# A transformer block in float32: second token shift summed from ScalarE's outputs, unpadded LoRA row tiles, new instruction orders

## The reference, cut to what matters

```
xn  = ln(x);  sx = prev token of xn - xn
xxx = tanh((xn + sx*maa_x) @ maa_w1)            # 5 groups of 32
x5  = xn + sx*(maa_stack + xxx @ maa_w2)        # 5 mixtures: k, w, v, r, g
w   = exp(-exp(time_decay + tanh(x5[1] @ decay_w1) @ decay_w2))
r, k, v = x5[3] @ Wr.T, x5[0] @ Wk.T, x5[2] @ Wv.T;  g = silu(x5[4] @ Wg.T)
att = scan over time of s = k v + w s, read with r and u
x   = x + (groupnorm(att) * g) @ Wo.T
xn2 = ln(x);  sx2 = prev token of xn2 - xn2     # first token of a sequence: a row of the state
xk  = xn2 + sx2*ffn_maa_k;  xr = xn2 + sx2*ffn_maa_r
x   = x + sigmoid(xr @ ffn_Wr.T) * (relu(xk @ ffn_Wk.T)^2 @ ffn_Wv.T)
```

## Time and profile before

| | |
|---|---|
| time of three runs | 520.23, 521.76, 522.25 us; median 521.76 |
| span of the profiled execution | 520.3 us, first to last instruction |
| median less span | 1.46 us, what lies around the span and the spread of the runs |
| PE / DVE / ACT / POOL busy | 479.2 / 474.4 / 281.7 / 101.6 us |
| mean granted TensorE clock | 0.987 of full speed |

### The profile page before, as it was taken

One profiled execution on the slowest core, in us unless ns is written; L12 is line 12 of the kernel. 1 busy time (PEld: TensorE's weight loads), 2 busy tenths in 40 slices (PEclk: granted clock), 3 DMA queues, 4 the chain that ended last, 5 costly groups with the idle time before them and its releaser, 6 DMA issues. The chain is left out here.

```text
span 520.3 us, 6254 instructions
## 1 busy us (share of the span) xinstructions
PE 479.2 (92%) x2200; PEld 284.2 (55%) x2200; DVE 474.4 (91%) x528; ACT 281.7 (54%) x612; POOL 101.6 (20%) x93
## 2 busy tenths in 40 slices
...
DMA packets 26999, 69.49 MB, mean 134 GB/s; under 512 B 1624, under 2 KB 19928, under 8 KB 24536
## 3 DMA queue, kind: packets, MB, share of 16 engines
...
## 5 line engine op out<-in xcount | busy, mean ns | idle before, releaser
L630 DVE TENSOR_TENSOR_SCAN kv<-w_sb,kv 128x512 f32<-128x512 f32 (+2 forms) x144 | 146.6, 1084 | 0.1
L958 PE MATMUL pa<-x,large_sb 128*128 128x512 f32 (+2 forms) x272 | 115.2, 567 | 5.0 <-DVE x L545 2.9
L451 POOL COPY kv<-s_sb 128x32 f32<-128x32 f32 (+2 forms) x36 | 54.6, 1518 | 145.6 <-PE patt L1130 141.4
L958 PEld LDWEIGHTS pa<-x,large_sb 128*128 128x128 f32 x272 | 51.2, 194 | 57.5 <-issue 44.3
L620 DVE TENSOR_TENSOR kv<-vrep,k_sb 128x2016 f32<-128x2016 f32 (+2 forms) x34 | 70.1, 2064 | 3.3 <-issue 3.3
L638 DVE TENSOR_TENSOR kv<-kv,r_sb 128x2048 f32<-128x2048 f32 (+2 forms) x36 | 72.9, 2043 | 0.2
L536 DVE SCALAR_TENSOR_TENSOR x<-pb,vec_sb,sx 128x512 f32<-128x512 f32 (+1 forms) x64 | 42.7, 708 | 6.0 <-PE pb L1002 5.9
L420 POOL DMA_DIRECT2D x<-xn x21 | 20.0, 951 | 111.5 <-DVE x L536 111.5
L1130 PE MATMUL patt<-kv,const_sb 128*32 128x512 f32 (+2 forms) x288 | 34.7, 557 | 0.5 <-DVE kv L638 0.4
L1002 PE MATMUL pb<-th,w_sb 32*128 32x512 f32 (+2 forms) x100 | 33.3, 596 | 1.5 <-DVE x L536 1.5
L1156 PE MATMUL pc<-large_sb,att 128*128 128x256 f32 x120 | 32.0, 390 | 0.0
...
## 6 DMA issues: line engine op xcount, KB each, us to landing
...
x<-xn POOLq DMA_DIRECT2D x18, 512.0 KB, 8.3
...
x_tok<-in_x SPq DMA_DIRECT2D x6, 512.0 KB, 10.2
...
xres<-in_x SPq DMA_DIRECT2D x6, 512.0 KB, 10.7
out<-xres SPq DMA_DIRECT2D x6, 512.0 KB, 5.0
out<-trr POOLq DMA_DIRECT2D x6, 512.0 KB, 8.1
```

Of the source, the lines that this page charges most:

```text
L451: pool.tensor_copy(kv[:, q % 2, :, 0:nb, 0], s0_sb[:, half, G4 * j:G4 * (j + 1), FIRST[c]:FIRST[c] + nb]).then_inc(s0_put, 1)
L630: ins = dve.tensor_tensor_scan(flat, w_sb[:, p, q % HF, 0:nb].rearrange("p b t -> p (b t)"), flat, 0.0, ALU.mult, ALU.add)
L958: ins = pe.matmul(dst[:, m, 0:n], w(a)[:, m * P:(m + 1) * P], src[:, a, :], start=(a == 0), stop=(a == HF - 1))
```

## The change

`c_xn` now makes four tiles from the transposed norm in PSUM: for `xr` and for `xk` a part of the token itself (scale `ln2_w*(1 - m)`) and a part of the token before it (scale `ln2_w*m`, written one column later). That is eight ACTIVATEs in place of two and two small copies for the first tokens of the sequences. `c_shift` on DVE is one TENSOR_TENSOR that adds the two tiles of `xr`; for `xk` a DMA from POOL's queue adds them in SBUF (`add_shifted`, step ax), and KK waits for it; in the last three parts DVE adds `xk` too. The scale and bias vectors are made once on POOL (`make_vecs`, step mv, ten small instructions).

The fold of the fifth mixture goes from four quarters to two halves (`FOLD = 2`); the weights are no longer padded with zeros. X4 is four matmuls of 32 rows (`LORA`) and 256 columns, D2 four of 64 rows (`DECAY`) and 256 columns, and the two halves of the tokens go to different PSUM banks. All five order lists are replaced by lists that are written out in full. Because `k_shifted` lies where `xn2` lay and `r_shifted` lies in `sq`, xn2 now waits for Y2 of the chunk before. `load_v` waits for the stored v in both halves, since vl1 may now come first.

```diff
-FOLD, DFOLD = P // LORA, P // DECAY
+FOLD, DFOLD = 2, P // DECAY
...
-PE_ORDER = [("BO", 2), ("X2", 1), ("P0", 1), ("X3", 1), ("S0", 2), ("T2", 3), ("X4", 1), ("P1", 1), ("S1", 2),
-            ("RR", 3), ("D1", 1), ("KK", 3), ("D2", 1), ("P3", 1), ("Y2", 3), ("S2", 2), ("T1", 0), ("S3", 2),
-            ("CB", 1), ("VR", 2), ("P4", 1), ("W1", 0), ("X01", 0), ("WO", 2)]
...
-ACT_ORDER = [("tg", 2), ("th", 1), ("st", 0), ("st2", 3), ("v", 1), ("nrm2", 3), ("xn2", 3), ("k", 1),
-             ("rr", 3), ("nrm", 0), ("thd", 1), ("kk", 3), ("w", 1), ("r", 1), ("xn", 0), ("sq", 2),
-             ("rstd", 2)]
...
-PE_TAIL = [("WO", 7), ("BO", 8), ("S0", 8), ("T2", 7), ("S1", 8), ("RR", 7), ("S2", 8), ("KK", 7), ("S3", 8),
-           ("VR", 8), ("Y2", 7), ("WO", 8), ("WO", 9), ("WO", 10), ("T2", 8), ("T2", 9), ("RR", 8), ("T2", 10),
-           ("RR", 9), ("KK", 8), ("RR", 10), ("KK", 9), ("KK", 10), ("Y2", 8), ("Y2", 9), ("Y2", 10)]
-ACT_TAIL = [("r", 8), ("w", 8), ("sq", 7), ("rstd", 7), ("st2", 7), ("nrm2", 7), ("xn2", 7), ("tg", 8),
...
+DVE_STEPS = """
+    st1.0 nrm1.0 shift.0 cwv.0 mix0.0 mix1.0 mix2.0 mix3.0 cs0.0 a0.0 a1.0 sc0.0 mix4.0 shift.1 rk.0 rs0.0 sc1.0
+    bonus.0 mix0.1 a2.0 mix1.1 rs1.0 mix2.1 sc2.0 mix3.1 rs2.0 a3.0 mix4.1 sc3.0 rk.1 rs3.0 a0.1 bonus.1 shift.2
+    sc0.1 a1.1 gate.0 mix0.2 mix1.2 sc1.1 mix2.2 rs0.1 rs1.1 mix3.2 a2.1 mix4.2 shift2.0 sc2.1 a3.1 rs2.1 sc3.1
...
+    mix3.6 mix4.6 rs1.5 a2.5 shift2.4 a3.5 sc2.5 rs2.5 sc3.5 rs3.5 rk.6 out.4 shift.7 a0.6 bonus.6 gate.5 sc0.6
+    mix0.7 mix1.7 a1.6 rs0.6 sc1.6 mix2.7 a2.6 mix3.7 rs1.6 shift2.5 mix4.7 a3.6 sc2.6 rs2.6 sc3.6 rs3.6 rk.7
+    out.5 a0.7 shift.8 bonus.7 sc0.7 gate.6 a1.7 mix0.8 mix1.8 sc1.7 mix2.8 rs0.7 mix3.8 rs1.7 a2.7 a3.7
+    shift2.6 sc2.7 mix4.8 rs2.7 sc3.7 rs3.7 a0.8 out.6 sc0.8 rk.8 a1.8 bonus.8 gate.7 rs0.8 sc1.8 rs1.8 a2.8
+    a3.8 sc2.8 rs2.8 sc3.8 rs3.8 shift2.7 gate.8 gate.9 st2.8 gate.10 nrm2.8 out.7 st2.9 nrm2.9 st2.10 shift2.8
+    nrm2.10 shift2.9 shift2.10 out.8 out.9 out.10
+"""
+PE_STEPS = """
+    T1.0 W1.0 X01.0 X2.0 X3.0 P0.0 P1.0 D1.0 VS.0 D2.0 T1.1 X4.0 P3.0 P4.0 W1.1 CB.0 X01.1 BO.0 S0.0 P0.1 X2.1
+    P1.1 X3.1 S1.0 D1.1 X4.1 P3.1 D2.1 T1.2 S2.0 CB.1 S3.0 VR.0 P4.1 W1.2 X01.2 WO.0 BO.1 X2.2 P0.2 X3.2 T2.0
+    S0.1 S1.1 X4.2 P1.2 RR.0 D1.2 KK.0 P3.2 D2.2 Y2.0 S2.1 T1.3 S3.1 CB.2 VR.1 P4.2 W1.3 X01.3 WO.1 BO.2 X2.3
+    P0.3 X3.3 T2.1 S0.2 P1.3 X4.3 S1.2 D1.3 RR.1 D2.3 P3.3 KK.1 T1.4 CB.3 Y2.1 S2.2 S3.2 P4.3 W1.4 VR.2 X01.4
+    P0.4 X2.4 WO.2 P1.4 X3.4 BO.3 S0.3 D1.4 T2.2 X4.4 P3.4 S1.3 S2.3 D2.4 RR.2 T1.5 KK.2 P4.4 Y2.2 S3.3 CB.4
+    VR.3 W1.5 X01.5 WO.3 P0.5 X2.5 BO.4 T2.3 X3.5 P1.5 X4.5 S0.4 S1.4 D1.5 RR.3 D2.5 P3.5 KK.3 S2.4 T1.6 CB.5
+    Y2.3 S3.4 P4.5 VR.4 W1.6 X01.6 WO.4 X2.6 P0.6 X3.6 P1.6 T2.4 X4.6 BO.5 S0.5 D1.6 S1.5 P3.6 RR.4 T1.7 KK.4
+    D2.6 S2.5 Y2.4 S3.5 CB.6 VR.5 P4.6 W1.7 BO.6 X01.7 WO.5 X2.7 P0.7 S0.6 T2.5 X3.7 P1.7 X4.7 S1.6 D1.7 RR.5
+    D2.7 KK.5 P3.7 Y2.5 S2.6 T1.8 S3.6 CB.7 VR.6 P4.7 W1.8 X01.8 WO.6 P0.8 X2.8 BO.7 X3.8 T2.6 S0.7 S1.7 P1.8
+    X4.8 RR.6 D1.8 KK.6 S2.7 D2.8 Y2.6 S3.7 P3.8 VR.7 CB.8 BO.8 WO.7 S0.8 S1.8 T2.7 P4.8 S2.8 S3.8 RR.7 VR.8
+    KK.7 WO.8 Y2.7 WO.9 T2.8 WO.10 T2.9 RR.8 T2.10 KK.8 RR.9 RR.10 KK.9 KK.10 Y2.8 Y2.9 Y2.10
+"""
+ACT_STEPS = """
+    st.0 xn.0 th.0 st.1 nrm.0 nrm.1 v.0 thd.0 k.0 w.0 xn.1 st.2 r.0 tg.0 th.1 nrm.2 v.1 k.1 thd.1 r.1 w.1 xn.2
+    sq.0 rstd.0 tg.1 th.2 st.3 st2.0 nrm2.0 v.2 xn2.0 k.2 rr.0 thd.2 nrm.3 kk.0 r.2 w.2 xn.3 sq.1 rstd.1 tg.2
+    th.3 st.4 st2.1 nrm2.1 v.3 xn2.1 k.3 nrm.4 thd.3 rr.1 r.3 w.3 kk.1 xn.4 st.5 sq.2 tg.3 th.4 rstd.2 v.4 nrm.5
+    st2.2 k.4 nrm2.2 thd.4 xn2.2 w.4 r.4 rr.2 xn.5 kk.2 sq.3 tg.4 rstd.3 th.5 st2.3 nrm2.3 v.5 xn2.3 k.5 thd.5
+    st.6 rr.3 w.5 r.5 nrm.6 kk.3 xn.6 sq.4 tg.5 rstd.4 th.6 st.7 st2.4 v.6 nrm2.4 k.6 xn2.4 thd.6 nrm.7 r.6 rr.4
+    kk.4 xn.7 w.6 sq.5 rstd.5 tg.6 th.7 st.8 nrm.8 st2.5 v.7 nrm2.5 xn2.5 k.7 thd.7 rr.5 kk.5 w.7 r.7 xn.8 sq.6
+    rstd.6 tg.7 th.8 st2.6 nrm2.6 nrm2.8 v.8 xn2.6 k.8 rr.6 thd.8 kk.6 w.8 sq.7 r.8 rstd.7 st2.7 nrm2.7 xn2.7
+    sq.8 tg.8 rr.7 rstd.8 kk.7 st2.8 st2.9 xn2.8 st2.10 xn2.9 rr.8 xn2.10 rr.9 kk.8 rr.10 kk.9 kk.10
+"""
+POOL_STEPS = """
+    rd1.0 rd1.1 s00.0 s01.0 ad3.0 ad1.0 rd1.2 ad4.0 ad1.1 s02.0 s03.0 s00.1 s01.1 mv.0 rd1.3 ad3.1 ad1.2 rd2.0
+    ad3.2 s02.1 ax.0 ad4.1 s03.1 ad4.2 s00.2 s01.2 rd1.4 ad1.3 rd2.1 ad0.0 ad3.3 ay.0 s02.2 ax.1 ad4.3 s03.2
+    ad0.1 s00.3 s01.3 rd1.5 ad1.4 ay.1 rd2.2 ad3.4 s02.3 ax.2 s03.3 ad4.4 s00.4 ad1.5 s01.4 ay.2 ad0.2 rd2.3
...
-        kk_buf, xhat2, sx2, e_buf = sq, ob, sq, mix
+        kk_buf, xhat2, e_buf = sq, ob, mix
+        k_shifted, r_shifted = xn2, sq
...
+            def add_shifted(k):
+                if k >= LAST:
+                    return
+                pool.wait_ge(xn2_ready, k + 1)
+                n = extent(k)[1]
+                pool.dma_start(xk[:, :, 0:n], k_shifted[:, :, 0:n], accum_op=ALU.add).then_inc(xk_added, 16)
...
+            def make_vecs(k):
+                pool.wait_ge(in_prev, 16)
+                pool.wait_ge(ln_put, 1)
+                for row, share in enumerate(("ffn_k", "ffn_r")):
+                    pool.tensor_tensor(prev2_sb[:, row], prev_sb[:, 0], both(share).unsqueeze(2).broadcast_to([P, HF, B]),
+                                       ALU.mult).then_inc(made_prev, 1)
+                for x in ("k", "r"):
+                    for of, end in (("ln2_w", ""), ("ln2_b", "_b")):
+                        pool.tensor_tensor(both(f"{x}_shifted{end}"), both(of), both(f"ffn_{x}"), ALU.mult).then_inc(made_vecs, 1)
+                pool.wait_ge(made_vecs, 4)
+                for x in ("k", "r"):
+                    for of, end in (("ln2_w", ""), ("ln2_b", "_b")):
+                        pool.tensor_tensor(both(f"{x}_own{end}"), both(of), both(f"{x}_shifted{end}"), ALU.subtract).then_inc(made_vecs, 1)
...
+            def mix_folds(c, n, a):
+                g, nt = MIXES[n], extent(c)[1]
+                nf = nt // FOLD
+                return dve.scalar_tensor_tensor(out=by_fold(x5[:, x5_slot(n), a, 0:nt]), in0=pb[:, :, a * nf:(a + 1) * nf],
+                                                scalar=vec(f"maa{g}", a), in1=by_fold(shifted(c)[:, a, 0:nt]), op0=ALU.add, op1=ALU.mult)
...
             def c_shift(k, _):
                 dve.wait_ge(xn2_ready, k + 1)
-                c, at, n = part(k)
-                first = FIRST[c] + at // L
-                seqs = [ap[:, :, span(k)].rearrange("p a (b t) -> p a b t", t=L) for ap in (sx2, xn2)]
+                dve.tensor_tensor(xr[:, :, span(k)], xr[:, :, span(k)], r_shifted[:, :, span(k)], ALU.add).then_inc(xr_ready, 1)
                 if k >= LAST:
-                    dve.wait_ge(y2_done, LAST)
-                dve.tensor_tensor(seqs[0][:, :, :, 0], prev_sb[:, 0, :, first:first + n // L], seqs[1][:, :, :, 0], ALU.subtract)
-                dve.tensor_tensor(seqs[0][:, :, :, 1:L], seqs[1][:, :, :, 0:L - 1], seqs[1][:, :, :, 1:L], ALU.subtract).then_inc(sx2_ready, 1)
-                dve.wait_ge(sx2_ready, k + 1)
-                for dst, name, done in ((xr, "ffn_r", xr_ready), (xk, "ffn_k", xk_ready)):
-                    for a in range(HF):
-                        ins = dve.scalar_tensor_tensor(out=dst[:, a, span(k)], in0=sx2[:, a, span(k)], scalar=vec(name, a),
-                                                       in1=xn2[:, a, span(k)], op0=ALU.mult, op1=ALU.add)
-                    ins.then_inc(done, 1)
+                    dve.tensor_tensor(xk[:, :, span(k)], xk[:, :, span(k)], k_shifted[:, :, span(k)], ALU.add).then_inc(xk_ready, 1)
...
-                act.activation(th[:, 1, 0:n // FOLD], pb[:, 1, 0:n // FOLD], ACT.Tanh).then_inc(th_ready, 1)
+                act.activation(th[0:FOLD * LORA, 1, 0:n // FOLD], pb[0:FOLD * LORA, 1, 0:n // FOLD], ACT.Tanh).then_inc(th_ready, 1)
...
-                for a in range(HF):
-                    ins = act.activation(e_buf[:, a, 0:n], acc(c, pc, pb)[:, a, 0:n], ACT.Exp, bias=vec("time_decay", a))
+                nf = n // DFOLD
+                for a in range(HF):
+                    ins = act.activation(by_fold(e_buf[:, a, 0:n]), acc(c, pc, pb)[:, :, a * nf:(a + 1) * nf], ACT.Exp, bias=vec("time_decay", a))
...
-                    act.wait_ge(xk_ready, ends(k))
-                n = part(k)[2]
-                for a in range(HF):
-                    ins = act.activation(xn2[:, a, span(k)], product(k)[:, a, 0:n], ACT.Identity, bias=vec("ln2_b", a), scale=vec("ln2_w", a))
+                    act.wait_ge(y2_done, ends(k))
+                if k == 0:
+                    act.wait_ge(made_vecs, 8)
+                    act.wait_ge(made_prev, 2)
+                c, at, n = part(k)
+                first, nb = FIRST[c] + at // L, n // L
+                for x, own, shifted, row in (("r", xr, r_shifted, 1), ("k", xk, k_shifted, 0)):
+                    heads = shifted[:, :, span(k)].rearrange("p a (b t) -> p a b t", t=L)
```

(29 more changed lines are left out.)

85 lines of the change are left out of this document (42 added, 43 removed), and 20 rows, old and new, of tables (ACT_HEAD, DVE_HEAD, PE_HEAD, POOL_HEAD).

## The result

The changed kernel took 555.1 us in the median of four runs (551.19 to 556.76), the kernel before 522.0 on the same chip. The ratio is 1.063, with an interval of 1.058 to 1.067. The forecast was 516.9 us with 503 to 530 as its range: wrong in sign, and the time is outside the range.

What follows compares the result with a forecast made beforehand. PE and DVE were both taken as full, with PE setting the middle's pace after the change. Terms -3 - 5.5 (PE's period) - 2 + 5 - 7.7 + 8.3 = -4.9 gave a 515.4 us span, forecast 516.9 us, range 503 to 530.

Steps and rivals of the forecast that it cites:

- The local costs: Durations of changed steps: X4 and D2 1.05 us each, shift2 1.2, xn2 6.1, the adding DMA's landing 7.5.
- I take 0 for this (bounds 0 and + 2 us a period): ACT's xn2, 4.6 us longer a chunk, was to delay PE by nothing through the steps behind it (k, thd, r).
- The page's rule: Skill page: put adds and multiplies on VectorE, not ScalarE; by it, moving the sums to ACT would be a loss.
- + 5: Middle: PE's KK waits for the adding DMA of xk, shortfalls over chunks 2 to 6 costing 5 us in all.
- Rival 2: KK's wait for the DMA is longer: at 12 us of landing + 23 in place of + 5, 535 us; chance 0.2.
- -3: Head, to 120 us: earlier centring of Wv and fewer X4.0 matmuls gain 3 us (bounds -6 and + 3).
- -2: Middle: a filler ahead of X01 in some chunks saves 2 of 5.2 us of tanh waits (bounds -5 and + 2).
- -7.7: From 430 us to the last S3, at DVE's pace: cheaper or moved shift2 and less idling gain 7.7 us (bounds -9 and 0).
- + 8.3: Tail after the last S3: 36.7 us against 28.4 through PE, ACT and last parts, 8.3 us lost (bounds + 4 and + 11).
- 4: Rival: the row tiles of X4 and D2 don't run side by side, + 0.5 a period instead of -1.0, 525 us; chance 0.05.
- 1: Rival: everything fits, the DMA lands before KK asks and PE runs at its 54.8 us floor, 502.6 us; chance 0.17.
- 3: Rival: the ends eat the gain, head 0 and tail + 11, the rest as forecast, 522.6 us; chance 0.13.

Runs made afterwards that it cites:

- run 5: The whole new computation in the old orders, with VectorE adding xk and no adding DMA, against the kernel before: 540.81 us, 1.040.
- run 10: New computation with VectorE adding xk, new orders for the head alone and old ones from there, against the kernel before: 539.15 us, 1.032.
- run 6: The changed kernel with its new orders kept, but xk added by VectorE instead of the DMA: 534.79 us, 1.025 to the kernel before.
- run 3: New orders with the old computation (old second shift, old padded tiles), against the kernel before: 542.67 us, 1.038.
- run 1: The kernel before with the unpadded row tiles alone, old orders and old second shift: 520.12 and 519.24 us undisturbed, median of all four 524.72.
- run 16: Repeated run of row tiles, old second shift and new orders for the head alone, against the kernel before: 518.96 us, 0.992.
- run 13: Row tiles and old second shift, with the new head orders kept one chunk longer, against the kernel before: 525.79 us, 1.002.
- run 14: Row tiles and old second shift, with the new orders at both head and end, against the kernel before: 527.86 us, 1.001.
- run 11: run 10 with one more semaphore, so VectorE can add xr while ScalarE makes the k half: 534.83 us, 1.022 to the kernel before.
- run 12: run 11 with the second shift of the last chunk's three parts computed the old way: 527.06 us, 1.009 to the kernel before.

## Why the prediction was wrong, point by point

- **What bounds the kernel:** right. Both full engines had no room, and VectorE's saved 21 us bought nothing. What the reading lacked: with PE full, the new waits are not taken up by slack elsewhere.
- **The local costs:** right. D2 and X4 take 1.07 and 1.06 us (8 rows each; the modelled row adds a little), the adds 1.22 us, ScalarE's stage 5.6 to 6 us, the landing of the DMA 7.2 us in the median (4.4 to 13.1):

```profile
106.83 1.14 PE L1124 MATMUL pb<-thd,dw_sb 64*128 64x256 f32 x8
143.36 1.13 PE L1075 MATMUL pb<-th,w_sb 32*128 32x256 f32 x8
```

- **"I take 0 for this (bounds 0 and + 2 us a period)", ScalarE's longer stage:** failed in the old orders. It was followed to k, thd and r behind xn2, not to `xr`: by the one signal at the end of all ten instructions `xr` is ready 6.9 us behind the start of the stage instead of 4.9, and RR starts at 7.0 instead of 6.1. It measured 1.8 us a chunk in runs 5 and 10, some 11 us in all in the middle, close to the upper bound. In the changed kernel itself it isn't the loss: RR stands later there, its waits for `xr` on this tile sum to 2.4 us, and under the new orders shift and row tiles together gain 8 us (run 6 against 3).
- **The page's rule** (the Trainium skill, "ScalarE: Activation LUTs", section "Rules for kernel authors") that speaks against sums on ScalarE was dismissed because ACT had 18 us idle. Runs 1 and 5 show that it held in the old orders, where not ACT's throughput but its latency was on the path; in the new orders no run shows a price.
- **"+ 5" for KK's wait:** the step that failed most plainly. 6.3 us of it stand in the trace, and yet the DMA costs 20 (555.1 against run 6's 534.8). The term was sized by that wait alone. It left out the mixture's DMA issued next, which in chunk 4 lands after 17.2 us instead of 6.2, P4, which the new order asks for soon after it, and the clock behind the wait. Of the two traces' difference of 13.3 us (the fastest execution of the one, the slowest of the other) chunk 4 has 10.9. How the 20 us divide among these isn't shown. Rival 2 named the DMA but put the price at KK, and its 535 us was still 20 too low.
- **The orders, "-3", "-2" and "-7.7":** the second step that failed. Together they forecast a gain of 12.7 us; measured is a gain of 6 under the new shift (run 6 against 5) and a loss of 20 under the old one (run 3). The head gave 9.9 us in this trace, more than its bound of 6, and 5.6 in run 16's; whether it stays to the end isn't shown. The middle of the lists was counted as free but for two waits; run 13 shows 5 us for the one chunk tried, run 14 some 5 for the end, run 3 some 20 in all. The last scans gave 4.6 of the 7.7.
- **The clock:** no term at all. Waits were counted at their length.
- **"+ 8.3" for the tail:** right in kind, + 10.6 measured from the last scan. Of it 4.7 us are ScalarE's longer parts (runs 11 and 12), and the orders alone make 8.5 (run 3; the two share their waits). VR.8 stands behind RR.7 on PE, so the first gate begins 13.7 us after the last scan instead of 9.6, and WO.9 starts 4.8 us after WO.8, behind Y2.7, where before it came 1.3 us after (500.95 and 502.24 us in that timeline):

```profile
521.06 0.61 DVE L684 SCALAR_TENSOR_TENSOR att<-patt,vec_sb,rstd 128x128 f32<-128x128 f32 x2 [9.50 <-ACT rstd L919]
523.54 0.59 PE L1194 MATMUL pa<-xres,const_sb 128*128 128x256 f32 x2
524.83 3.62 PE L1003 MATMUL pc<-large_sb,sq 128*128 128x256 f32 x16
528.29 0.59 PE L1194 MATMUL pb<-xres,const_sb 128*128 128x256 f32 x2
```

- **The rivals:** 4 is refuted by the rows above and by run 1; 1 and 3 by the total. Without the term for KK the forecast's sum is 9.9 us below the kernel before, and run 6, without that DMA, is 13 us above it: the loss would have been missed with KK's wait priced right, too.

In sum, from the row tiles on: + 21 us for the shift (run 5), - 6 for the new orders under it (run 6), + 20 for the DMA. On the other way the orders come to + 20 with the old shift (run 3), and shift and row tiles together to - 8 under them (run 6 against 3). The parts don't add up independently: what the new orders cost depends on the shift they are laid out for. Why they cost 20 with the one and gain 6 with the other is not settled; a list laid out for the old shift's latencies wasn't made.
